# Flamingo block in fp32, one core: who writes the pieces of the probabilities, who computes the rows' factors, and when two groups' norms are transposed

## The reference, cut to what matters

```python
x = x + tanh(g_xattn[0]) * L0_xattn(layernorm(x), ctx)   # 32 heads of 128, 8 kv heads, q and k RMS-normed
x = x + tanh(g_ffn[0])   * L0_ffn(layernorm(x))          # router over 8 experts, rank 16
x = x + tanh(g_xattn[1]) * L1_xattn(layernorm(x), ctx)   # 16 heads of 96, 4 kv heads
x = x + tanh(g_ffn[1])   * L1_ffn(layernorm(x))          # silu(x Wg) * (x Wu) Wd, 1792 wide
# attention, each: q from x, k and v from [context, x]; per head
scores = q @ k.T * scale                 # 128 queries x 256 keys
probs  = exp(scores - max) / sum(exp(scores - max))
out    = probs @ v ; y = out @ Wo
```

## Time and profile before

| | |
|---|---|
| median of 3 runs | 1402.43 us (1400.9 to 1403.67) |
| profiled execution | 1396.48 us, of which the span is 1394.4 us |
| mean granted clock of TensorE | 0.979 |
| PE, PEld busy | 94%, 83% |
| DVE, ACT, POOL busy | 74%, 49%, 36% |
| chain that ended last | PE 71%, DVE 17%, ACT 4%, issue 4% |

### The profile page before, as it was taken

One profiled execution on the slowest core, in us unless ns is written; L12 is line 12 of the kernel. 1 busy time (PEld: TensorE's weight loads), 2 busy tenths in 40 slices (PEclk: granted clock), 3 DMA queues, 4 the chain that ended last, 5 costly groups with the idle time before them and its releaser, 6 DMA issues.

```text
span 1394.4 us, 24169 instructions
## 1 busy us (share of the span) xinstructions
PE 1312.8 (94%) x7776; PEld 1150.6 (83%) x7776; DVE 1030.9 (74%) x2620; ACT 680.4 (49%) x2354; POOL 508.2 (36%) x808
## 2 busy tenths in 40 slices
PE   7899999999999999999999888899999998579998
PEld 6788888888888888888887777788888888468887
DVE  5688777777787787777778877888888888533433
ACT  5456665555565566556664433355444543222221
POOL 2445544554455355445544423133223332300000
PEclk8999999999999999999999999999999999789999
DMA  6233332332332332323333211242433322740000
GB/s 189 56 82 76 60 85 62 75 91 46 83 82 46 91 76 61 83 60 73 87 62 68 51 31 31 61 88 58 84 65 72 79 46 47 210 136 1 31 0 31
DMA packets 233439, 98.11 MB, mean 70 GB/s; under 512 B 204800, under 2 KB 217600, under 8 KB 233344
## 3 DMA queue, kind: packets, MB, share of 16 engines
q1 hardware_dynamic: 210416, 58.75, 21.7%
q10 hardware_dynamic: 18992, 27.28, 6.5%
q0 software_dynamic: 3936, 11.01, 2.6%
HBM read 39.08 MB, written 2.10 MB: 30 GB/s over the span
## 4 chain that ended last, share of the span: by engine, by line
PE 71%; DVE 17%; ACT 4%; issue 4%; POOL 2%; DMA 2%; DVEq 0%; SPq 0%; POOLq 0%; ACTq 0%
PE bank L467 18%; PE bank L469 18%; PE bank L468 18%; PE bank L692 7%; DVE split L938 5%; PE bank L678 4%; DVE mx L1012 3%; PE bank L546 3%; DMA turned<-pieces 2%; ACT split L706 2%; DVE pieces L1041 1%; PE bank L536 1%; ACT scratch L760 1%; DVE x L1054 1%; DVE scratch L960 1%
## 5 line engine op out<-in xcount | busy, mean ns | idle before, releaser
L467 PE MATMUL bank<-split 128*128 128x256 f32 (+6 forms) x2120 | 716.7, 338 | 15.5 <-issue 7.2
L469 PE MATMUL bank<-split 128*128 128x256 f32 (+6 forms) x2120 | 696.5, 329 | 0.0
L468 PE MATMUL bank<-split 128*128 128x256 f32 (+6 forms) x2120 | 695.9, 328 | 0.0
L467 PEld LDWEIGHTS bank<-split 128*128 128x128 f32 (+2 forms) x2120 | 405.4, 191 | 48.9 <-issue 10.3
L469 PEld LDWEIGHTS bank<-split 128*128 128x128 f32 (+2 forms) x2120 | 404.6, 191 | 36.4 <-issue 0.2
L468 PEld LDWEIGHTS bank<-split 128*128 128x128 f32 (+2 forms) x2120 | 405.9, 191 | 28.2
L706 ACT ACTIVATE split<-bank 128x512 fp32r<-128x512 f32 (+7 forms) x456 | 194.4, 450 | 325.5 <-PE bank L546 264.0
L1249 POOL CAST split<-turned 128x512 fp32r<-128x512 f16 x384 | 227.9, 622 | 333.9 <-DMA turned<-pieces 333.9
L938 DVE TENSOR_TENSOR split<-bank,split 128x512 fp32r<-128x512 f32 (+7 forms) x456 | 228.0, 503 | 144.0 <-ACT split L706 140.1
L1041 DVE SCALAR_TENSOR_TENSOR pieces<-scratch,rs,pieces 128x256 f16<-128x256 f32 x384 | 180.4, 511 | 0.0
L760 ACT ACTIVATE scratch<-bank,nb,rq 128x256 f32<-128x256 f32 x256 | 141.8, 561 | 63.9 <-DVE nb L1017 63.8
(11 more groups left out here) (69 smaller groups left out, 1135.3 us busy)
## 6 DMA issues: line engine op xcount, KB each, us to landing
raw<-in_wq_a ACTq DMA_DIRECT2D x14, 512.0 KB, 3.6
raw<-in_wo_a ACTq DMA_DIRECT2D x14, 512.0 KB, 3.4
raw<-in_wkv_a ACTq DMA_DIRECT2D x7, 512.0 KB, 3.4
split<-in_gate_t POOLq DMA_DIRECT2D x2, 1792.0 KB, 7.6
split<-in_up_t POOLq DMA_DIRECT2D x2, 1792.0 KB, 11.2
turned<-pieces SPq DMA_TRANSPOSE x192, 3.1
raw<-in_wq_c ACTq DMA_DIRECT2D x8, 384.0 KB, 3.3
split<-in_down_t POOLq DMA_DIRECT2D x1, 2816.0 KB, 10.6
```

Source lines behind the costliest of these rows:

```text
L467: pe.matmul(out, whi, mhi, start=start, stop=False)
L468: pe.matmul(out, whi, mlo, start=False, stop=False)
L469: return pe.matmul(out, wlo, mhi, start=False, stop=stop)
```

## The change

1. `split_probs` is divided among three engines. POOL's new `sums_inverse` scales the sums and raises them to the power -1; ACT's new `probs_high` writes the high pieces as a Copy with the factor as its scale; DVE's `probs_low` keeps the low pieces.
2. `q_squares` reads the copy `qn` in SBUF in place of bank 6, and `q_turn` waits no longer for it.
3. `norm_turn` of norms 0 and 3 (first group of L0, last of L1) stands behind `k_turn` on PE; `norm_scale` of them stands behind `kv_low` on DVE, `norm_hi` behind `k_evac` on ACT, `norm_low` behind `probs_low(one, 1)`.

```diff
@@ PE @@
             def q_turn(L, g, b):
                 s = attn[L.name]
                 pe.wait_ge(s.qcp_done, count(g, b, 1, 1))
-                if L.normed:
-                    pe.wait_ge(s.qsq_done, count(g, b, NH, NH))
...
-                if beside_norm is not None:
-                    if beside_norm[0] == 1:
-                        wait_prior(pe, *prev, lambda s: s.yadd_done, 1)
+                if beside_norm is not None and beside_norm[0] == 1:
+                    wait_prior(pe, *prev, lambda s: s.yadd_done, 1)
                     norm_turn(*beside_norm)
                 if two is not None:
                     q_proj(*two)
                     k_turn(*two)
+                if beside_norm is not None and beside_norm[0] != 1:
+                    norm_turn(*beside_norm)
@@ ACT @@
             def q_squares(L, g, b):
                 s, hd = attn[L.name], L.hd
                 if L.normed:
+                    act.wait_ge(s.qcp_done, count(g, b, 1, 1))
                     for h in range(NH):
-                        act.activation(bank[3][:, h * hd:(h + 1) * hd], bank[6][:, h * hd:(h + 1) * hd], ACT.Square,
+                        act.activation(bank[3][:, h * hd:(h + 1) * hd], qn[:, h * hd:(h + 1) * hd], ACT.Square,
...
+            def probs_high(L, g, b, i):
+                s = attn[L.name]
+                act.wait_ge(s.rs_done, count(g, b, 2, i + 1))
+                wait_prior(act, L, g, b, lambda s: s.turned[i], 16)
+                for h in range(2):
+                    n = 2 * i + h
+                    act.activation(piece[:, i, 0, h, :], probs[:, n, :], ACT.Copy, scale=rs[:, n:n + 1]
+                                   ).then_inc(s.pa_done, 1)
...
+                if one is not None:
+                    probs_high(*one, 0)
+                if two is not None:
+                    q_evac(*two)
+                if one is not None:
+                    probs_high(*one, 1)
+                if two is not None:
+                    k_evac(*two)
                 if beside_norm is not None and beside_norm[0] != 1:
                     norm_hi(*beside_norm)
-                if two is not None:
-                    q_evac(*two)
-                    k_evac(*two)
@@ DVE @@
-            def split_probs(L, g, b, i):
-                s = attn[L.name]
-                pr = slice(2 * i, 2 * i + 2)
-                dve.wait_ge(s.exp_done, count(g, b, NH, 2 * i + 2))
-                dve.tensor_scalar(sums_in[:, pr], sums[:, pr], 1.0 / PSCALE, None, ALU.mult).then_inc(s.sc_done, 1)
-                dve.wait_ge(s.sc_done, count(g, b, 2, i + 1))
-                dve.reciprocal(rs[:, pr], sums_in[:, pr]).then_inc(s.rs_done, 1)
-                dve.wait_ge(s.rs_done, count(g, b, 2, i + 1))
-                wait_prior(dve, L, g, b, lambda s: s.turned[i], 16)
-                for h in range(2):
-                    n = 2 * i + h
-                    dve.tensor_scalar(piece[:, i, 0, h, :], probs[:, n, :], rs[:, n:n + 1], None, ALU.mult
-                                      ).then_inc(s.pa_done, 1)
+            def probs_low(L, g, b, i):
+                s = attn[L.name]
                 for h in range(2):
                     n = 2 * i + h
                     dve.wait_ge(s.pa_done, count(g, b, NH, n + 1))
...
-                if beside_norm is not None:
+                if beside_norm is not None and beside_norm[0] == 1:
                     norm_scale(*beside_norm)
...
                 if two is not None:
                     kv_low(*two)
+                if beside_norm is not None and beside_norm[0] != 1:
+                    norm_scale(*beside_norm)
...
                 if one is not None:
-                    split_probs(*one, 0)
+                    probs_low(*one, 0)
                 if two is not None:
                     k_low(*two)
...
-                if beside_norm is not None and beside_norm[0] != 1:
-                    norm_low(*beside_norm)
                 if lora is not None:
                     lora_low(lora)
                 if one is not None:
-                    split_probs(*one, 1)
+                    probs_low(*one, 1)
+                if beside_norm is not None and beside_norm[0] != 1:
+                    norm_low(*beside_norm)
@@ POOL @@
+            def sums_inverse(L, g, b, i):
+                s = attn[L.name]
+                pr = slice(2 * i, 2 * i + 2)
+                pool.wait_ge(s.exp_done, count(g, b, NH, 2 * i + 2))
+                pool.tensor_scalar(sums_in[:, pr], sums[:, pr], 1.0 / PSCALE, None, ALU.mult).then_inc(s.sc_done, 1)
+                pool.wait_ge(s.sc_done, count(g, b, 2, i + 1))
+                pool.tensor_tensor(rs[:, pr], sums_in[:, pr], minus_one[:, 0:2], ALU.pow).then_inc(s.rs_done, 1)
...
                 if new_kvq is not None:
                     kv_lo(*group_of(new_kvq), 0)
+                if one is not None:
+                    sums_inverse(*one, 0)
+                if new_kvq is not None:
                     kv_lo(*group_of(new_kvq), 1)
                 if new_o:
-                    for c in range(1, L.oc):
+                    o_lo(L, g, 1)
+                if one is not None:
+                    sums_inverse(*one, 1)
+                if new_o:
+                    for c in range(2, L.oc):
                         o_lo(L, g, c)
```

More of the change, by code:

```diff
@@ L272, in build @@
         half_neg = sb("half_neg", NH)
+        minus_one = sb("minus_one", 2)
+        sums_in = sb("sums_in", NH)
         gates = sb("gates", 4)
@@ L293, in build @@
         rs = sb("rs", NH)
-        sums_in = sb("sums_in", NH)
         lg = sb("lg", 2 * EXPERTS)
@@ L645, in step @@
                     q_turn(*two)
-            pe.wait_ge(consts, 3)
+            pe.wait_ge(consts, 4)
             awake(22)
@@ L912, in _ @@
             exps(L0, 0, 0, 1)
+            probs_high(L0, 0, 0, 0)
+            probs_high(L0, 0, 0, 1)
             kv_evac(L0, 0, 1)
@@ L1171, in _ @@
             norm_low(0, 2)
-            split_probs(L0, 0, 0, 0)
-            split_probs(L0, 0, 0, 1)
+            probs_low(L0, 0, 0, 0)
+            probs_low(L0, 0, 0, 1)
             kv_low(L0, 0, 1)
@@ L1325, in _ @@
             pool.memset(hd_eps[:, :], RMS_EPS * L0.hd).then_inc(consts, 1)
+            pool.memset(minus_one[:, :], -1.0).then_inc(consts, 1)
             pool.wait_ge(ident_zero, 1)
@@ L1328, in _ @@
                                pattern=[[-1, P]], channel_multiplier=1).then_inc(consts, 1)
-            pool.wait_ge(consts, 3)
+            pool.wait_ge(consts, 4)
             norm_rstd(0, 0)
@@ L1334, in _ @@
             norm_rstd(0, 2)
+            sums_inverse(L0, 0, 0, 0)
+            sums_inverse(L0, 0, 0, 1)
             k_norm(L0, 0, 1)
```

## The result

Changed kernel: 1420.89 us (median of 4 runs, 1420.23 to 1423.12). Kernel before in the same session: 1401.92 us (1400.90 to 1403.67). Ratio 1.0137, 95% interval 1.0119 to 1.0154: slower, by 19.0 us, and the whole interval lies above 1. I had forecast 1418 and a change of +15.3.

The account below looks back on a forecast made before the run. PE was taken as the bound, busy 553.34 of 555 us in L0's middle groups. Terms +6.6 +2.0 +14.0 -5.0 -2.3 = +15.3 us gave 1418 us by the median (1411.8 from the profiled execution); range 1397 to 1430.

Parts of the forecast that it names:

- Ordinary steps cost nothing: Ordinary L0 steps: ACT's added high pieces fit within slack of 0.8 and 1.1 us, so the cost is nothing.
- Rival B: Ordinary steps break: `k_evac` behind `probs_high(1)` costs 0.3 us beyond slack in 55 steps, +17: 1435 us; chance 0.07.
- Step b = 1 of L0: L0 groups 1 to 6: POOL's inverses delay its Wo chunks, stalling PE 1.1 us a group, 6.6 us.
- Last L0 group: Step b = 1 there: POOL also splits router weights, no slack is left, both inverses count: 2.0 us.
- Steps b = 5 and 6: L0 groups 0 to 6: late `qt_evac` and POOL queue stall PE 2.0 us a group, 14.0 us, the largest term.
- Rivals A and D: A: slack suffices, only gains stay, 1395 us, chance 0.13. D: heavy steps cost half, +4, 1406 us, chance 0.20.
- First group: L0's first group: moved norms and freed squares shorten PE's waits, a gain of 5 us, bounds 2 and 10.
- Last L1 group: Four steps that wait for the norm reach their values earlier, 0.58 us each, a gain of 2.3 us.
- L1 b = 1: Step b = 1 of the four L1 groups: taken as 0, bounds -0.7 and +0.7 us each.
- rival C: New stalls lower TensorE's clock in half of 13 heavy steps, +10: 1428 us; chance 0.10.

Follow-up runs that it names:

- e6: Changed kernel, but VectorE does the whole split in steps b = 1 and b = 5 of the L0 groups: 1387.96 us.
- e10: Changed kernel, but VectorE does the whole split in L0's first group and in steps b = 1 and 5 of all groups: 1386.48 us.
- e8: Changed kernel, but VectorE writes the high pieces; GpSimd still computes the factors: 1405.71 us.
- e7: Changed kernel, but VectorE computes the factors, ahead of its first low piece; ScalarE still writes the high pieces: 1394.10 us.
- e11: Changed kernel, but ScalarE's two high pieces of the q weights (step b = 5) stand behind `qt_evac` and `o_evac`: 1416.74 us.
- e2: Kernel before plus the moved norms alone (part 3); squares as before, whole split on VectorE: 1387.08 us.
- e4: Kernel before plus the squares and norms changes (parts 2 and 3), whole split on VectorE: 1388.67 us.
- e9: Changed kernel, but with the old split, all on VectorE, in the first group of L0 alone: 1415.05 us.
- e3: Kernel before plus the squares change alone (part 2); norms as before, whole split on VectorE: 1400.65 us.
- e12: As e4, but ScalarE's two high pieces of the q weights (step b = 5) stand behind `qt_evac` and `o_evac`: 1395.21 us.

## Why the prediction was right

Its main steps held, and most costs were taken too small.

1. **Ordinary steps cost nothing**: held exactly, 11.84 and 11.84; e6 and e10 show it apart from the rest. The ScalarE copy was 503 ns in place of 479, a pair 0.81 us to the next start in place of 0.78, and still fitted. Rival B falls.
2. **Step b = 1 of L0, 6.6 us**: the mechanism is right (e8 has it, e7 hasn't), the size was 8.9. I counted GpSimd's delay against PE's slack of 1.04 us and got 1.1; the chunks were 0.91 us late in two pieces, and the cost of stopping PE twice, 0.57, was missing. Last L0 group: 2.0 predicted, 2.7 measured.
3. **Steps b = 5 and 6, 14.0 us**: three stalls in the places named: `kv_proj` for `k_low` (0.45 predicted, 0.74), POOL's `q_lo(1)` (0.6, 0.61), `k_turn` for DVE behind the collision of its weight lows with GpSimd's. `k_turn` moved by 2.89 in place of 2.0, and seven groups came to 19.3. I had added no price for a stop beyond its wait: 2.38 us of brackets made 3.26 over an ordinary step, of which the kernel before already paid 0.36. e7 and e8 with one half each cost 0.8 and 1.0, and the rest comes with both. With 1.5 in step b = 1 the groups lie 4.4 us further apart, for about 3 predicted, and PE's share of the middle is 96.9% as named. Rivals A and D, that slack absorbs all or half, fall.
4. **First group, -5**: this is the step that failed. The changed kernel's trace gained nothing there (+0.5 without step b = 6), e11's 2.4. The gain from the norms is real, and larger, with the old split (e2 -11 us in all, e4 -8.4 in the first group). What I left out is that the divided split costs something in this group too, although I had named GpSimd's queue as the cause of its waits: e9 prices that at 2 to 4 us beside step b = 6. It is not the inverses alone (e8), and the mechanism stays open. The squares, of which I had credited a part, give nothing by themselves (e3). Against e3, whose time is near the median of before, the changed kernel would be 2.3 us ahead in this stretch, so about half of the forecast gain is missing, or all of it, by which trace of the old order one takes.
5. **Last L1 group, -2.3**: 0.53 us a step, -2.1.
6. **L1 b = 1, 0 with bounds of 0.7**: 0.65 each, at the edge of the bound; it stays in e8 (12.0) and is gone in e7 (11.2), so it is the inverses.
7. **Clock, rival C**: the granted clock of the middle is 1.00 as before, so its 10 us are not there. What it describes happened once in the first group instead (0.72 from 84 to 88 us, above).

So the terms for the heavy steps were some 8.3 us too small (L0) and the first group up to 5.5 us too kind, and L1's steps b = 1 added 1.9. The errors point the same way, and by the rows the change costs 31.2 us, twice the forecast. That the whole came out at 19.0 for 15.3 by medians is partly luck: the profile of before that I had measured from was a fast one, and the stretches that I set at nothing came out shorter by 6 us in the changed kernel's trace.

On the rule of the Trainium skill ("Perfetto Trace Analysis", "Optimizing Scalar/DVE Operations"), that work shifted between GpSimd and VectorE may not help as they share a port: for wide operations the traces agree (VectorE's two weight lows last 2.56 us where they overlap GpSimd's, 1.87 in e11, where they overlap it less). The inverses acted through the order of GpSimd's queue, and e8's loss in step b = 1 needs no port: two inverses are 2 us ahead of the last chunk.

## What to carry to other kernels

When a chain is divided among engines, look at each receiving queue in its busiest step, not in its mean: here six steps in eight took the work for nothing, and the other two lost more than the change could give. Two halves of a division can cost more together than their sum (5.4 and 17.0 us here, 32.2 with both), so test them apart and together. When a full PE must stop, count each stop at more than its visible wait, and test the parts of a bundled change apart: one of these three was worth 11 us, one nothing, and one cost about 30.

## What the runs showed of the hardware

- In these traces a stop of TensorE costs more than the trace's bracket. Matmuls of 128x512 start 0.23 us apart and are busy 0.39; the first after a wait was busy 0.50 and its successor started 0.34 behind it. Two waits of 0.63 and 0.28 lengthened a step by 1.48.
- A small VectorE operation can end just when a wide GpSimd operation ends. `nb` over 128x2, 0.16 us later in the same step, took 1.08 in e11 and ended at 416.95, GpSimd's weight low above at 416.93; in e12 the two ended at 403.44 and 403.42. The hold seems to go the other way too: the two casts above took 2.09 us beside two wide VectorE operations that read `raw`, and the next two casts of that step 1.17. Rows of VectorE in e11:

```profile
413.36 1.87 DVE L961 TENSOR_TENSOR split<-raw,split 128x512 fp32r<-128x512 f32 x2
...
415.87 1.08 DVE L1040 SCALAR_TENSOR_TENSOR nb<-mx,rq 128x2 f32<-128x2 f32 x1
```
- The pow of the inverses on GpSimd is 0.70 to 0.85 us over 128x2, that of q's factors mostly 1.01 over 128x4, up to 1.13, where VectorE's reciprocal over 128x2 takes 0.17.
